# Router output rows kept by partition, loaded with one transfer per group, and added by VectorE alone

## The chip, the cores and the metric

The kernel runs on one core of a Trainium2 chip. The metric is the device time of one execution in microseconds (us); of several runs the median counts. Below, PE is TensorE (matrix products), DVE is VectorE, ACT is ScalarE, POOL is GpSimd and SP is SyncE, which here only issues transfers (DMAs).

## What is computed

The block works on 2048 tokens (8 sequences of 256) of width 128, in float32:

```
x = x + 0.5 * ffn(layernorm(x))        # layer 0: 8 experts, each token goes to 2 of them
x = x + mamba(layernorm(x))            # projections, a short convolution, a scan over time
x = x + 0.5 * ffn(layernorm(x))        # layer 1: the same experts
```

Inside `ffn` a router picks the two best of 8 experts for each token and gives each a weight. With hact = up * gelu(gate), the result of a token is the weighted sum of the two chosen experts' outputs:

```
probs = softmax(x @ gate_w.T); topw, sel = top_k(probs, 2); topw = topw / sum(topw)
out   = sum over the 2 choices of  topw * (hact @ down_w[expert].T)
```

## The kernel before

**Layout.** Token t = 128 c + p lies in partition p and chunk c, so `x` is [128 partitions, 16 chunks, 128]. Four chunks make a group (GROUPS = 4, GC = 4); a group of one tensor is 128 x 512 float32, 256 KB.

**The expert stage.** `route` (DVE, L1033) sorts the 4096 (token, choice) pairs by expert into NT = 39 tiles of 128 places, some of them padding. It builds one-hot matrices; PE (`onehot`, L755) multiplies them with a small constant table (`K_BLOCK`, `K_P`) and gets for each place the block number and the partition of its token. L1093 to L1095 make two row numbers from them: `put_i`, the row of the scratch tensor `expert_rows` in DRAM to which the place's result goes (a number beyond the tensor for padding, which is dropped), and `get_i`, the row of the scratch tensor `xn_rows` in DRAM from which its input comes. SP writes the normalised tokens to `xn_rows` (L327). In `ffn`, POOL issues for each tile one indirect gather (L378, up to six tiles ahead) and one indirect scatter (L386); PE, ACT and DVE do the tile between them. In DRAM, row 128 c + p of `xn_rows` is the token's, and row 2048 k + 128 c + p of `expert_rows` is its choice k: neighbouring rows belong to neighbouring partitions.

**The return.** When all scatters of a layer have landed (L334), SP issues eight loads (L337), for each group g the rows of choice 0 and then those of choice 1, 256 KB each, in runs of 512 bytes. They land in `ybuf[g]`, which shares its space with `ring_space` (groups 0 to 2) and `gate` (group 3); profile rows carry those names. Then ACT scales choice 0 with its weight (L499, four instructions), POOL scales choice 1 (L405, one instruction), and DVE adds both to `x` (L1167, two instructions, the second waits for the first).

**What follows.** After layer 0 DVE's own order is written out by hand: add group 0, statistics of group 0 (L1007 to L1012), add group 1, normalise group 0 (L1023), statistics of group 1, and so on. PE starts matrix products that only keep its clock up (`keep_clock`, L694) when group 0 of `x` is updated, then turns the normalised group 0 (L701), and after ACT's copy (L465) starts the input projection (L865). POOL's queue holds the scalings of layer 0 between its `rsqrt` steps (L363). After layer 1 each group of `x` is stored to the output as soon as it is updated (L340), and the kernel ends.

Of the kernel before, what the change touches and what calls it, by code (L numbers as in the profile page):

```python
# [18 lines left out]
ALU = mybir.AluOpType  # L19
ACT = mybir.ActivationFunctionType  # L20
# [8 lines left out]
P = 128  # L29
B, L, D = 8, 256, 128  # L30
T = B * L
C = T // P
GROUPS, GC = 4, C // 4
GT = GC * P
E, F, TOPK = 8, 512, 2
FC = F // P
J = TOPK * C
NT = (T * TOPK - E) // P + E
# [41 lines left out]
K_BLOCK = K_TILE + NT  # L80
K_P = K_BLOCK + J
# [37 lines left out]
def macaron_block(nc, x_in, experts_in, consts_in, vectors_in, mats_in, out):  # L119
    with ExitStack() as ctx:  # L120
# [3 lines left out]
        def sem(name):  # L124
            return ctx.enter_context(nc.semaphore(name))

        xn_dram = [nc.dram_tensor(f"xn_rows_{l}", (T, D), F32).ap() for l in range(2)]
        y_dram = [nc.dram_tensor(f"expert_rows_{l}", (TOPK * T, D), F32).ap() for l in range(2)]

        ps = ctx.enter_context(nc.psum_tensor("ps", [P, 8, 512], F32))  # L130
# [26 lines left out]
        x = sb("x", [P, C, D])  # L157
# [23 lines left out]
        half_w = sb("half_w", [P, TOPK, C])  # L181
# [18 lines left out]
        put_f = sb("put_f", [P, NT])  # L200
        put_i = sb("put_i", [P, NT], I32)
# [14 lines left out]

        ids = sb("ids", [P, NT])
        gate = sb("gate", [P, T])
        ybuf = [rows.rearrange("p (k c d) -> p k c d", k=TOPK, c=GC) for rows in
                [ring_space[:, i * TOPK * GT:(i + 1) * TOPK * GT] for i in range(3)] + [gate[:, 0:TOPK * GT]]]  # L220

        delta = xn[:].rearrange("p c d -> p (c d)")
# [42 lines left out]
        h_turned, hT_ready = sem("h_turned"), sem("hT_ready")  # L265
        down_done, y_ready = sem("down_done"), sem("y_ready")
        y_loaded = [sem(f"y_loaded_{g}") for g in range(GROUPS)]
        y_scaled = [sem("y_scaled_by_act"), sem("y_scaled_by_pool")]
        x_moved = sem("x_moved")

        xz_done, silu_done, gate_ready = sem("xz_done"), sem("silu_done"), sem("gate_ready")
# [13 lines left out]
        def spread(ap, axis, shape):  # L285
            return ap.unsqueeze(axis).to_broadcast(shape)
# [10 lines left out]
        def grp(g):  # L297
            return slice(g * GC, (g + 1) * GC)
# [12 lines left out]
        @block.sync  # L311
        def _(sp):
            for g in range(GROUPS):
                sp.dma_start(x[:, grp(g), :], x_in[:, grp(g), :]).then_inc(x_loaded[g], 16)
                if g == 1:
                    sp.dma_start(consts[:], consts_in).then_inc(consts_in_s, 16)
            sp.dma_start(mats[:], mats_in).then_inc(mats_in_s, 16)
            for e in range(EARLY_EXPERTS):
                sp.dma_start(w_lo[:, e, :].bitcast(F32), experts_in[:, e, 0:GU]).then_inc(w_loaded[e], 16)

            for l in range(2):
                rows = xn_dram[l].rearrange("(c p) d -> p c d", p=P)
                y_rows = y_dram[l].rearrange("(k c p) d -> p k c d", k=TOPK, p=P)
                for g in range(GROUPS):

                    wait_normalised(sp, 2 * l, g)
                    sp.dma_start(rows[:, grp(g), :], xn[:, grp(g), :]).then_inc(xn_stored[g], 16)  # L327
                if l == 0:
                    for e in range(EARLY_EXPERTS, E):
                        sp.dma_start(w_lo[:, e, :].bitcast(F32), experts_in[:, e, 0:GU]).then_inc(w_loaded[e], 16)  # L330
                    sp.dma_start(w_down[:], experts_in[:, :, GU:WCOLS]).then_inc(down_loaded, 16)
                    sp.dma_start(vectors[:], vectors_in).then_inc(vectors_in_s, 16)
                for r in range(RING):
                    sp.wait_ge(scattered[r], 16 * (l + 1) * PER_SLOT[r])  # L334
                for g in range(GROUPS):
                    for k in range(TOPK):
                        sp.dma_start(ybuf[g][:, k], y_rows[:, k, grp(g), :]).then_inc(y_loaded[g], 16)  # L337
            for g in range(GROUPS):
                sp.wait_ge(x_moved, GROUPS + g + 1)
                sp.dma_start(out[:, grp(g), :], x[:, grp(g), :]).then_inc(stored, 16)  # L340
            sp.wait_ge(stored, 16 * GROUPS)
# [3 lines left out]
        def _(pool):  # L345
# [53 lines left out]
                    if t >= PUT_AFTER:  # L399
                        put(t - PUT_AFTER)  # L400

            def scale_experts(l, g):

                pool.wait_ge(y_loaded[g], 16 * TOPK * (l + 1))
                pool.tensor_tensor(ybuf[g][:, 1], ybuf[g][:, 1],  # L405
                                   spread(half_w[:, 1, grp(g)], 2, [P, GC, D]), ALU.mult).then_inc(y_scaled[1], 1)

            def mamba():
                scale_experts(0, 0)
                scale_experts(0, 1)  # L410
                rsqrt(1, 0)
                scale_experts(0, 2)
                rsqrt(1, 1)
                scale_experts(0, 3)
                rsqrt(1, 2)
                rsqrt(1, 3)

                pool.wait_ge(setup_copied, 3)
                pool.wait_ge(xn_ready, FIRST_ON_ACT + GROUPS)
                pool.tensor_tensor(x[:], x[:], spread(out_c[:], 1, [P, C, D]), ALU.add).then_inc(cb_added, 1)  # L420
                pool.wait_ge(cb_added, 1)
                for q in range(DVE_DELTAS, GROUPS):
                    cols = slice(q * GT, (q + 1) * GT)
                    pool.wait_ge(log_done, q + 1)
                    pool.wait_ge(pos_done, q + 1)
                    pool.tensor_tensor(delta[:, cols], delta[:, cols], soft[:, cols], ALU.add
                                       ).then_inc(pool_delta_ready, 1)
                    pool.wait_ge(pool_delta_ready, q - DVE_DELTAS + 1)
                    pool.tensor_tensor(gate[:, cols], gate[:, cols], delta[:, cols], ALU.mult).then_inc(pool_dg_ready, 1)
                    pool.wait_ge(pool_dg_ready, q - DVE_DELTAS + 1)  # L430

                def step(k, n, ring_new):
                    pool.wait_ge(h_ready, k + 1)
                    pool.wait_ge(c_copied, k + 1)
                    if not ring_new:
                        pool.wait_ge(hc_summed, k - 3)
                    pool.tensor_tensor(hc[:, n % 4, :], hs[:, n % 4, :], c_row[:, n % 4, :],  # L437
                                       ALU.mult).then_inc(hc_ready, 1)

                for n in range(N):  # L440
                    step(n, n, n < 4)
                with pool.Fori(1, GROUPS) as q:
                    for n in range(N):
                        step(q * N + n, n, False)
# [9 lines left out]
            for g in range(GROUPS):  # L454
                rsqrt(2, g)
            ffn(1)
            for g in range(GROUPS):
                scale_experts(1, g)


        @block.scalar
        def _(act):
# [31 lines left out]

            def scale_experts(l, g):

                act.wait_ge(y_loaded[g], 16 * TOPK * (l + 1))
                for c in range(GC):
                    i = nc.scalar.activation(ybuf[g][:, 0, c, :], ybuf[g][:, 0, c, :], ACT.Copy,  # L499
                                             scale=half_w[:, 0, g * GC + c:g * GC + c + 1])  # L500
                i.then_inc(y_scaled[0], 1)

            def load_table(function, i):

# [492 lines left out]
        def _(dve):  # L997
            order = [0]

            def chain(ins):  # L1000
                order[0] += 1
                ins.then_inc(dve_order, 1)
                dve.wait_ge(dve_order, order[0])
# [29 lines left out]
            def route(l):  # L1033
# [56 lines left out]
                dve.tensor_scalar(weights_i[:], exp_f[:], float(E - 1), None, ALU.min)  # L1090

                dve.wait_ge(onehot_used, (l + 1) * GROUPS)
                chain(dve.tensor_scalar(put_f[:], ps[:, 4, 0:NT], float(P), float((J + 1) * P), ALU.mult, ALU.add))  # L1093
                chain(dve.tensor_tensor(put_i[:], put_f[:], ps[:, 4, NT:2 * NT], ALU.add))
                dve.tensor_scalar(get_i[:], put_i[:], T - 1, None, ALU.bitwise_and).then_inc(index_ready, 1)  # L1095

            def second_weights(l):

# [63 lines left out]

            def add_experts(l, g):

                for k in range(TOPK):
                    dve.wait_ge(y_scaled[k], l * GROUPS + g + 1)
                    i = dve.tensor_tensor(x[:, grp(g), :], x[:, grp(g), :], ybuf[g][:, k], ALU.add)  # L1167
                    if k == 0:
                        chain(i)
                i.then_inc(x_moved, 1)  # L1170
                dve.wait_ge(x_moved, l * GROUPS + g + 1)

            def mamba():
# [167 lines left out]
def _constants():  # L1341

    import numpy as np

    k = np.zeros((P, K_COLS), np.float32)
    i = np.arange(P)
    k[:, K_IOTA:K_IOTA + P] = i
    k[:, K_TRI:K_TRI + P] = i[:, None] < i[None, :]
    k[:, K_CENTRE:K_CENTRE + P] = np.eye(P) - 1.0 / P
    k[:, K_IDENT:K_IDENT + P] = np.eye(P)  # L1350
    k[:, K_TILE:K_TILE + NT] = P * np.arange(NT)
    k[:, K_BLOCK:K_BLOCK + J] = np.arange(J) - (J + 1)
    k[:, K_P] = i
    k[:, K_SEL:K_SEL + 2 * N] = (i[:, None] % (2 * N)) == np.arange(2 * N)
    return k

# [28 lines left out]
```

## Time and profile before

| | us |
|---|---|
| median of 3 runs | 534.25 |
| lowest, highest | 532.2, 536.88 |
| the profiled execution | 536.45 |
| its span in the trace | 534.3 |
| PE busy | 445.2 (83%) |
| DVE busy | 309.5 (58%) |
| POOL busy | 276.9 (52%) |
| ACT busy | 253.5 (47%) |

The shares are means over stages with different limits. Layer 0's experts fill about 43 to 172 us, the Mamba block about 172 to 352 us, layer 1's routing and experts about 352 to 517 us, and the last 17 us are the return of layer 1. Only a stretch of the chain that ended last sets the time.

### The profile page before, as it was taken

What the parts mean: (1) busy time and instruction counts of PE and PEld (TensorE: products, weight loads), DVE (VectorE), ACT (ScalarE), POOL (GpSimd) and SP (SyncE); (2) the same over time, 40 slices, a digit from 0 to 9 for tenths busy, and PEclk for the clock granted to TensorE, in tenths of its full rate; (3) what the DMA queues carried; (4) which work ended last, traced back from release to release, by engine and by line L of the source; (5) the groups of instructions that cost most, each with busy time, mean ns of one, the idle gap of its engine ahead of it and who ended that gap; (6) DMA issues with size and microseconds to landing.
All of it is one profiled execution on the core that took longest, in us unless ns stands there. A gap on an engine that the chain in (4) does not pass through costs nothing.

```text
span 534.3 us, 8797 instructions
## 1 busy us (share of the span) xinstructions
PE 445.2 (83%) x2131; PEld 289.2 (54%) x2132; DVE 309.5 (58%) x813; ACT 253.5 (47%) x579; POOL 276.9 (52%) x257
## 2 busy tenths in 40 slices
PE   6977999999997499499898989773989998899940
PEld 3755877787786144032222222422578786777840
DVE  5574433343343654799999999768233443333415
ACT  4474444444354415966666666352134453344413
POOL 3016666666633440377777767630456646665333
PEclk9579999999999589779999999966689999999985
DMA  8901111111200500000000000020011101112026
GB/s 293 373 21 44 40 42 40 42 35 37 41 18 10 157 1 2 0 1 0 2 0 1 0 0 0 2 79 1 25 35 43 45 25 42 36 36 37 23 56 187
DMA packets 21465, 25.01 MB, mean 47 GB/s; under 512 B 3517, under 2 KB 15812, under 8 KB 21440
## 3 DMA queue, kind: packets, MB, share of 16 engines
q1 hardware_dynamic: 16448, 15.39, 8.8%
q0 software_dynamic: 4992, 9.32, 6.6%
q8 instruction: 11, 0.18, 0.1%
q14 instruction: 14, 0.11, 0.1%
HBM read 17.35 MB, written 8.26 MB: 48 GB/s over the span
## 4 chain that ended last, share of the span: by engine, by line
PE 50%; DVE 16%; issue 10%; ACT 10%; another core or an unknown queue 5%; DMA 4%; POOL 2%; SPq 1%; ACTq 0%; DVEq 0%; POOLq 0%
PE ps L817 11%; DVE ring_space L1255 9%; PE ps L788 6%; PE ps L808 6%; PE ps L790 6%; PE ps L789 5%; PE ps L865 3%; DMA ring_space<-expert_rows 2%; ACT shared L615 2%; PE ps L714 2%; PE ps L761 2%; POOL shared L437 2%; PE ps L701 2%; ACT hT L537 1%
## 5 line engine op out<-in xcount | busy, mean ns | idle before, releaser
L378 POOL DMA_INDIRECT xg<-xn_rows,get_i x78 | 80.4, 1031 | 102.8 <-DVE get_i L1095 49.0
L386 POOL DMA_INDIRECT expert_rows<-ysb,put_i x78 | 78.6, 1007 | 57.7 <-DVE ysb L1148 38.1
L1140 DVE TENSOR_TENSOR hidden<-ps,hidden 128x256 f32<-128x256 f32 x156 | 58.8, 418 | 79.2 <-ACT hidden L530 38.9
L437 POOL TENSOR_TENSOR shared<-ring_space,shared 128x512 f32<-128x512 f32 x64 | 82.6, 1292 | 30.9 <-DVE ring_space L1255 30.5
L530 ACT ACTIVATE hidden<-ps 128x256 f32<-128x256 f32 x156 | 52.0, 389 | 80.2 <-PE ps L790 70.1
L817 PE MATMUL ps<-w_down,hT 128*128 x624 | 85.7, 281 | 0.0
L915 PE MATMUL ps<-shared,consts 128*128 128x512 f32 x128 | 73.3, 655 | 9.5 <-POOL shared L437 7.4
L817 PEld LDWEIGHTS ps<-w_down,hT 128*128 128x128 f32 x624 | 76.5, 193 | 3.7 <-issue 0.9
L537 ACT COPY hT<-ps 128x512 f32<-128x512 f32 x78 | 45.7, 586 | 63.5 <-remote 37.6
L788 PE MATMUL ps<-w_hi,xT_hi 128*128 x156 | 68.9, 442 | 4.1 <-issue 3.6
L789 PE MATMUL ps<-w_lo,xT_hi 128*128 x156 | 61.8, 396 | 0.0
L790 PE MATMUL ps<-w_hi,xT_lo 128*128 x156 | 61.8, 396 | 0.0
L808 PE MATMUL ps<-consts,hidden 128*128 128x128 f32 x312 | 48.1, 277 | 10.8 <-ACT hT L537 8.0
L1131 DVE TENSOR_TENSOR xT_lo<-ps,xT_hi 128x128 fp32r<-128x128 f32 x78 | 22.7, 291 | 58.8 <-ACT xT_hi L523 55.5
L615 ACT COPY shared<-ps 128x512 f32<-128x512 f32 x64 | 37.5, 585 | 37.7 <-DVE ring_space L1255 35.4
L808 PEld LDWEIGHTS ps<-consts,hidden 128*128 128x128 f32 x312 | 36.9, 141 | 27.3 <-issue 14.3
L607 ACT ACTIVATE ps<-xn,neg_a 128x510 f32<-128x510 f32 (+1 forms) x64 | 44.5, 696 | 0.0
L915 PEld LDWEIGHTS ps<-shared,consts 128*128 128x128 f32 x128 | 20.3, 194 | 35.5 <-POOL shared L437 32.7
L1255 DVE TENSOR_TENSOR_SCAN ring_space<-ps,ring_space 128x512 f32<-128x512 f32 x32 | 38.9, 1216 | 0.9 <-ACT ps L607 0.9
L1255 DVE TENSOR_TENSOR_SCAN ring_space<-ps,hidden 128x512 f32<-128x512 f32 x32 | 38.8, 1215 | 0.0
L1148 DVE COPY ysb<-ps 128x128 f32<-128x128 f32 x78 | 22.4, 288 | 24.9 <-PE ps L817 19.5
L788 PEld LDWEIGHTS ps<-w_hi,xT_hi 128*128 128x128 f32 x156 | 29.6, 190 | 13.1 <-issue 9.3
(156 smaller groups left out, 609.5 us busy)
## 6 DMA issues: line engine op xcount, KB each, us to landing
w_lo<-in_experts SPq DMA_DIRECT2D x8, 512.0 KB, 7.7
ring_space<-expert_rows SPq DMA_DIRECT2D x12, 256.0 KB, 4.5
xn_rows<-xn SPq DMA_DIRECT2D x8, 256.0 KB, 3.3
w_down<-in_experts SPq DMA_DIRECT2D x1, 2048.0 KB, 11.8
xg<-xn_rows,get_i POOLq DMA_INDIRECT x78
expert_rows<-ysb,put_i POOLq DMA_INDIRECT x78
x<-in_x_rows SPq DMA_DIRECT2D x4, 256.0 KB, 5.1
gate<-expert_rows SPq DMA_DIRECT2D x4, 256.0 KB, 5.4
```

What stands on the lines that cost most here:

```text
L378: pool.indirect_dma_start(out=xg[:, r, :], out_offset=None, in_=xn_dram[l], in_offset=bass.IndirectOffsetOnAxis(ap=get_i[:, t:t + 1].bitca ...
L386: pool.indirect_dma_start(out=y_dram[l], in_=ysb[:, t % RING, :], in_offset=None, out_offset=bass.IndirectOffsetOnAxis(ap=put_i[:, t:t + 1 ...
L437: pool.tensor_tensor(hc[:, n % 4, :], hs[:, n % 4, :], c_row[:, n % 4, :], ALU.mult).then_inc(hc_ready, 1)
L530: nc.scalar.activation(gelu[:, slot % 2, half], ps[:, GATE_BANK[slot % 2], half], ACT.Gelu).then_inc(gelu_done, 1)
L788: pe.matmul(acc, xT_hi[:, slot % 3, :], hi, start=True, stop=False)
L789: pe.matmul(acc, xT_hi[:, slot % 3, :], lo, start=False, stop=False)
L790: return pe.matmul(acc, xT_lo[:, slot % 3, :], hi, start=False, stop=True)
L808: m = pe.transpose(ps[:, HT_BANK, f * P:(f + 1) * P], hact[:, slot % 2, f * P:(f + 1) * P], ident)
L817: m = pe.matmul(ps[:, RESULT_BANK[slot % 2], 0:D], hT[:, slot % 3, f * P:(f + 1) * P], flat_down[:, bass.ds(expert + f * D, D)], start=(f ...
L915: pe.matmul(y_bank(q), ident, hc[:, n % 4, :], start=(n == 0), stop=(n == N - 1)).then_inc(hc_summed, 1)
L1140: dve.tensor_tensor(hact[:, slot % 2, half], ps[:, UP_BANK[slot % 2], half], gelu[:, slot % 2, half], ALU.mult).then_inc(hact_done, 1)
L1255: dve.tensor_tensor_scan(hs[:, n % 4, :], ps[:, DECAY_BANK + n % 2, :], bx[n % 4], 0.0, ALU.mult, ALU.add).then_inc(h_ready, 1)
```

## The change

Both scratch tensors number their rows by partition first: row 16 p + c of `xn_rows`, and row 32 p + 2 c + k of `expert_rows`. A partition's rows of a group are then one run of 2 KB in the first and one of 4 KB, both choices together, in the second. The eight loads of a layer become four of 512 KB. `ybuf[g]` is ordered chunk, choice, column. The constants and L1093 to L1095 are changed so that the row numbers come out in the new order, with as many instructions as before. POOL's scalings are gone. DVE does choice 1 itself: for each chunk one instruction multiplies the row with its weight and adds it to `x` (four of 128 x 128), and then one 128 x 512 addition takes choice 0, scaled by ACT as before. Between these two DVE waits for the first four.

```diff
-        ybuf = [rows.rearrange("p (k c d) -> p k c d", k=TOPK, c=GC) for rows in
+        ybuf = [rows.rearrange("p (c k d) -> p c k d", k=TOPK, c=GC) for rows in
...
-                rows = xn_dram[l].rearrange("(c p) d -> p c d", p=P)
-                y_rows = y_dram[l].rearrange("(k c p) d -> p k c d", k=TOPK, p=P)
+                rows = xn_dram[l].rearrange("(p c) d -> p c d", p=P)
+                y_rows = y_dram[l].rearrange("(p c k) d -> p c k d", k=TOPK, p=P)
...
-                    for k in range(TOPK):
-                        sp.dma_start(ybuf[g][:, k], y_rows[:, k, grp(g), :]).then_inc(y_loaded[g], 16)
+                    sp.dma_start(ybuf[g], y_rows[:, grp(g)]).then_inc(y_loaded[g], 16)
...
-            def scale_experts(l, g):
-
-                pool.wait_ge(y_loaded[g], 16 * TOPK * (l + 1))
-                pool.tensor_tensor(ybuf[g][:, 1], ybuf[g][:, 1],
-                                   spread(half_w[:, 1, grp(g)], 2, [P, GC, D]), ALU.mult).then_inc(y_scaled[1], 1)
-
             def mamba():
-                scale_experts(0, 0)
-                scale_experts(0, 1)
                 rsqrt(1, 0)
-                scale_experts(0, 2)
                 rsqrt(1, 1)
-                scale_experts(0, 3)
...
-                act.wait_ge(y_loaded[g], 16 * TOPK * (l + 1))
+                act.wait_ge(y_loaded[g], 16 * (l + 1))
...
-                chain(dve.tensor_scalar(put_f[:], ps[:, 4, 0:NT], float(P), float((J + 1) * P), ALU.mult, ALU.add))
-                chain(dve.tensor_tensor(put_i[:], put_f[:], ps[:, 4, NT:2 * NT], ALU.add))
-                dve.tensor_scalar(get_i[:], put_i[:], T - 1, None, ALU.bitwise_and).then_inc(index_ready, 1)
+                chain(dve.tensor_scalar(put_f[:], ps[:, 4, NT:2 * NT], float(J), float(J * P), ALU.mult, ALU.add))
+                chain(dve.tensor_tensor(put_i[:], put_f[:], ps[:, 4, 0:NT], ALU.add))
+                dve.tensor_scalar(get_i[:], put_i[:], 1, T - 1, ALU.logical_shift_right, ALU.bitwise_and).then_inc(index_ready, 1)
...
-                for k in range(TOPK):
-                    dve.wait_ge(y_scaled[k], l * GROUPS + g + 1)
-                    i = dve.tensor_tensor(x[:, grp(g), :], x[:, grp(g), :], ybuf[g][:, k], ALU.add)
-                    if k == 0:
-                        chain(i)
-                i.then_inc(x_moved, 1)
+                dve.wait_ge(y_loaded[g], 16 * (l + 1))
+                for c in range(GC):
+                    at = g * GC + c
+                    i = dve.scalar_tensor_tensor(out=x[:, at, :], in0=ybuf[g][:, c, 1, :], scalar=half_w[:, 1, at:at + 1],
+                                                 in1=x[:, at, :], op0=ALU.mult, op1=ALU.add)
+                i.then_inc(second_added, 1)
+                dve.wait_ge(second_added, l * GROUPS + g + 1)
+                dve.wait_ge(y_scaled, l * GROUPS + g + 1)
+                dve.tensor_tensor(x[:, grp(g), :], x[:, grp(g), :], ybuf[g][:, :, 0, :], ALU.add).then_inc(x_moved, 1)
...
-    k[:, K_BLOCK:K_BLOCK + J] = np.arange(J) - (J + 1)
-    k[:, K_P] = i
+    k[:, K_BLOCK:K_BLOCK + J] = np.arange(J).reshape(C, TOPK).T.reshape(J)
+    k[:, K_P] = i - P
```

## Rows read from the trace of the kernel before

**Rows 1.** Chain of waits, 164 to 224 us; columns: start us, us, what.
```profile
170.28 2.13 DMA expert_rows<-ysb,put_i
...
172.53 0.38 SPq L337
...
180.73 0.70 DVE x L1167
...
182.19 1.73 DVE xn L1023 x4
...
185.75 6.74 PE ps L865 x8
```

**Rows 2.** Timeline, 160 to 192 us; start us, us, engine, line, operation, count, idle before.
```profile
176.31 1.28 ACT L499 ACTIVATE ring_space<-ring_space,half_w 128x128 f32<-128x128 f32 x4 [4.38 <-DMA ring_space<-expert_rows]
...
177.62 1.42 DVE L1167 TENSOR_TENSOR x<-x,ring_space 128x512 f32<-128x512 f32 x2 [5.71 <-ACT ring_space L499]
179.07 0.87 DVE L1007 BATCH_NORM_STATS2 stats<-x 128x6 f32<-128x128 f32 x4
...
179.09 4.02 PE L694 MATMUL ps<-ones_b 128*128 128x512 bf16 x9 [7.51 <-DVE x L1167]
...
180.39 0.17 DVE L1012 TENSOR_SCALAR var_e<-mv 128x4 f32<-128x4 f32 x1
180.64 1.04 POOL L363 TENSOR_TENSOR rstd<-var_e,neg_half 128x4 f32<-128x4 f32 x1
...
181.67 1.38 POOL L405 TENSOR_TENSOR ring_space<-ring_space,half_w 128x512 f32<-128x512 f32 x1
...
188.05 1.11 DVE L1023 TENSOR_SCALAR xn<-x,mv,rstd 128x128 f32<-128x128 f32 x4
```

**Rows 3.** Chain of waits, 505 us to the end.
```profile
515.29 2.11 DMA expert_rows<-ysb,put_i
...
525.56 0.70 DVE x L1167
...
526.29 1.42 DVE x L1167
...
527.73 1.48 DVE x L1167
...
530.68 0.69 DVE x L1167
```

**Rows 4.** Timeline, 506 us to the end.
```profile
521.73 1.28 ACT L499 ACTIVATE ring_space<-ring_space,half_w 128x128 f32<-128x128 f32 x4 [9.10 <-DMA ring_space<-expert_rows]
...
526.00 1.15 POOL L405 TENSOR_TENSOR ring_space<-ring_space,half_w 128x512 f32<-128x512 f32 x1 [0.65 <-DMA ring_space<-expert_rows]
...
527.61 1.04 POOL L405 TENSOR_TENSOR gate<-gate,half_w 128x512 f32<-128x512 f32 x1 [0.46 <-DMA gate<-expert_rows]
```

**Rows 5.** Windows: stretch, length, busy of each engine, PEclk, DMA share, GB/s.
```profile
8.00:11.00 3.00, 0.63 (x4) 0.42 (x4) 2.59 (x19) 2.49 (x7) 2.27 (x3) 1.00 1.03 414
...
172.50:174.00 1.50, 0.00 (x0) 0.00 (x0) 0.00 (x0) 0.00 (x0) 0.00 (x0) 1.00 0.05 16
174.00:175.00 1.00, 0.00 (x0) 0.00 (x0) 0.00 (x0) 0.00 (x0) 0.00 (x0) 0.91 1.02 307
175.00:176.00 1.00, 0.00 (x0) 0.00 (x0) 0.00 (x0) 0.00 (x0) 0.00 (x0) 0.50 1.05 276
...
190.00:192.00 2.00, 2.00 (x4) 0.53 0.00 0
...
382.00:384.00 2.00, 2.00 (x9) 0.74 (x6) 0.00 (x0) 0.00 (x0) 1.39 (x3) 0.74 0.11 33
...
100.00:160.00 60.00, 57.69 (x358) 47.77 (x357) 23.95 (x77) 26.25 (x76) 33.68 (x34) 1.00 0.14 34
```

**Rows 6.** One-line views of L1116 and L1255: durations in ns, min/median/max.
```profile
L1116 DVE TENSOR_SCALAR conv_rows<-mats,vectors x4: 277/315/477, 169.2 to 169.7; 128x128 f32<-128x128 f32 x4
...
L1255 DVE TENSOR_TENSOR_SCAN ring_space<-ps,ring_space x32: 1212/1216/1223, 224.2 to 332.9; 128x512 f32<-128x512 f32 x32
```

**Rows 7.** Page, costliest groups: busy us, mean ns, idle before with its releaser.
```profile
L378 POOL DMA_INDIRECT xg<-xn_rows,get_i x78 | 80.4, 1031 | 102.8 <-DVE get_i L1095 49.0
```

More of the change, by code:

```diff
@@ L267, in macaron_block @@
         y_loaded = [sem(f"y_loaded_{g}") for g in range(GROUPS)]
-        y_scaled = [sem("y_scaled_by_act"), sem("y_scaled_by_pool")]
+        y_scaled, second_added = sem("y_scaled"), sem("second_added")
         x_moved = sem("x_moved")
@@ L456, in _ @@
             ffn(1)
-            for g in range(GROUPS):
-                scale_experts(1, g)
         @block.scalar
@@ L495, in scale_experts @@
             def scale_experts(l, g):
-                act.wait_ge(y_loaded[g], 16 * TOPK * (l + 1))
+                act.wait_ge(y_loaded[g], 16 * (l + 1))
                 for c in range(GC):
-                    i = nc.scalar.activation(ybuf[g][:, 0, c, :], ybuf[g][:, 0, c, :], ACT.Copy,
+                    i = nc.scalar.activation(ybuf[g][:, c, 0, :], ybuf[g][:, c, 0, :], ACT.Copy,
                                              scale=half_w[:, 0, g * GC + c:g * GC + c + 1])
-                i.then_inc(y_scaled[0], 1)
+                i.then_inc(y_scaled, 1)
             def load_table(function, i):
```

## Prediction

> **What bounds the kernel now.** I read the page's chain of waits first: half of it is PE, and the scratch loads hold 2%. So the change can act on the path only where the chain passes through them, and I read the chain in detail at those two places, with the timeline beside it for the engines that are not in it.
>
> After layer 0 the chain runs from the last scatter into the loads, then ACT's scaling of group 1, DVE's additions, DVE's normalisation of group 0, and into PE's input projection at 185.75 [rows 1]. From there PE runs through the four groups with only ACT's short copies between, so whatever is won before 185.75 is won for the rest. After layer 1 the chain runs from the last scatter (landed 517.40) into the loads, ACT's scaling of group 1, and then DVE's additions one behind another until 531.37 [rows 3]; the last store and its landing follow.
>
> Two things are to be seen there. First, POOL and DVE slow each other: an addition of 128 x 512 takes 0.70 us, but two single ones that ran beside POOL's scalings took 1.42 and 1.48 [rows 3, 4]. In the same way the normalisation of group 0 took 1.73 beside POOL's scaling (1.38), the next one, mostly alone, 1.11 [rows 1, 2]. Second, the loads in 512-byte runs move 307 and 276 GB/s at their start, while 4 KB runs of the weights moved 414 at the kernel's start [rows 5].
>
> **The change part by part.**
>
> *Loads.* They are issued from 172.53; group 0's first bytes move some 1.35 us later, at about 173.9 (16 GB/s in the mean until 174.00, 307 from there) [rows 1, 5]. Its 0.524 MB take 1.81 us at 290 GB/s and 1.27 at 414, 0.54 less. The bounds are 0 and 0.54; I take 0.45, since the runs are as long as the weights' but strided differently. ACT started at 176.31 and 521.73 [rows 2, 4], so the new starts are 175.86 and 521.28. The later groups (2.10 MB in all) land by about 524.5 after layer 1 (518.85 + 2.10/0.40 + 0.4), or 526.3 at 300 GB/s. Fewer issues on SP cost nothing and free nothing: behind them SP only waits for the output.
>
> *The four new DVE instructions.* The trace has no such instruction on two 128 x 128 tensors. Four 128 x 128 statistics take 0.87 [rows 2]; four scalings with one per-partition factor take 0.93, read from the same timeline (mean start-to-start 0.22, one 0.315) [rows 6]; four with two factors take 1.11 [rows 2]. I take 1.05. Below that the floor is 0.87. The ceiling: the scan of 512 columns takes 1.216 against 0.70 for an addition [rows 1, 6], about 1 ns more per column; with that four would take 0.53 more, 1.58.
>
> The row nearest in kind speaks for one column per cycle (the addition, 0.70 for 512), the scan for two. The Trainium skill has a rule for it: Vector Engine (DVE) Microarchitecture Reference, "Points that are easy to get wrong", says that this instruction form with two SBUF sources that are not bf16 runs at half throughput. By the rule the sum would be the one of the first rival below; no instruction in this trace settles it.
>
> *DVE per group.* Before: 1.42 for two additions. After: 1.05, 0.04 for the wait, one addition 0.70, 0.04: 1.83. DVE has 0.41 more work per group, but no longer starts it after a scaling: the four begin when the load lands, beside ACT's 1.28. In the first group ACT ends last, so x is updated 1.28 + 0.03 + 0.70 = 2.0 after landing.
>
> *After layer 0.* Before: group 0 updated at 179.04 (177.62 + 1.42), statistics to 180.56, wait for ACT's group 1 until 180.73 (its scalings ended at 180.70), additions, normalisation 182.19 to 183.91 [rows 1, 2]. After: 175.86 + 2.0 = 177.87; statistics 1.50 to 179.37 (group 1 has landed by 177.2 even at 300 GB/s plus 0.6); 1.79 to 181.19; POOL's rsqrt, ready 1.1 after the statistics, at 180.5, is in time; normalisation 1.11 without POOL beside it, to 182.34. That is 1.57 earlier: 0.45 load, 0.72 one addition less in group 0, 0.61 the undisturbed normalisation, and -0.21 for group 1. What is next late is nothing on DVE: its later additions have cover, because PE's first projection lasts until 192.5 and needs group 1's normalised rows only then; DVE had them at 189.16 and has them at about 188.4. Were that cover gone, each group would cost 0.41.
>
> *After layer 1.* Start 521.28, first group 2.0 plus 0.03, three more at 1.83: 528.80. DVE sets the end, since all loads have landed before it asks for them. Before 531.37 [rows 3]; gain 2.57. In it are the two slowed additions (0.72 + 0.78 = 1.50).
>
> *Costed at nothing.* The writes of `xn_rows`: the gathers wait for the indices of DVE, not for them [rows 7]. Gathers and scatters in the new row order: POOL issues as many, and PE uses a gather six tiles, some 18 us, after its issue, against some 2.1 us in which a scatter lands [rows 1, 3]; DMA is busy 14% of the expert stage [rows 5]. Only a layer's first gather is nearer its use, where a few tenths could show. The last scatters of a layer (2.13 and 2.11 on the chain [rows 1, 3]) keep their price. Index arithmetic and one-hot products have as many instructions of the same size.
>
> **Sum.** 1.57 + 2.57 = 4.1 us. The profiled span goes from 534.3 to 530.2, its time from 536.45 to about 532.3. That execution lies 2.2 above the median; I subtract from the median: 534.25 - 4.1 = 530.1.
>
> **The rivals.**
>
> *The new instruction at half rate.* Then DVE needs 1.58 instead of 1.05 for the four, and in a first group 0.30 is all that is seen over ACT. Tail: 0.3 + 3 x 0.53 = 1.9 less gain; after layer 0: 0.3 + 0.53 = 0.8 less. Gain 1.4, time 532.9. For it: two operands from SBUF and the scan's row [rows 6]. Against: the addition also has two, at 0.70.
>
> *The clock rises sooner too.* PE starts its projection at half clock (granted 0.50; 0.53 in 190 to 192, so it rose at about 191.9, 6.1 us after 185.75) [rows 1, 5]. Eight instructions took 6.74 there. Before layer 1's experts PE was kept busy from 378.0 and the clock rose at about 383.0 (0.74 in 382 to 384), 5.0 later [rows 5]. With a projection that starts closer behind the `keep_clock` products (4.02 us [rows 2], so from 177.9 to 181.9; the turned group follows at 182.4), the rise may come 3 us sooner relative to the projection, worth half of that, 1.5. Gain 5.6, time 528.6. Against: the gap behind `keep_clock` stays, and where the rise falls may as well be chance.
>
> The Trainium skill (TensorE: Matmul & The Clock Gate, "Part 1") holds that where the rise falls differs from run to run; this trace's two delays, 6.1 and 5.0, agree. By that the forecast keeps its mean and gets wider.
>
> *Slower: the strided long runs load badly.* Every partition's 4 KB run begins 16 KB after its neighbour's. The tail ends at 518.85 + 2.10/rate + 0.4 + 2.0 once loads bind; that is 531.4 at 208 GB/s, where all of the tail's gain is gone. At 150 GB/s the tail loses 3.9 and the stretch after layer 0 0.4: 538.5. It decides from about 200 GB/s. For: nothing loads at this stride now. Against: 512-byte runs of the same tensor reach 276 and 307, long runs 414 [rows 5].
>
> The Trainium skill speaks for it in kind: DMA: Bandwidth & Descriptors, "Latency and other measured facts", gives 207 GB/s for row pitches of 512 KiB, fewer at larger ones, and nothing for 16 KiB. No run here shows it yet.
>
> *It does nothing.* Not possible in full: additions and scalings do leave the chain.
>
> **How the numbers follow.** Forecast 0.55 (its own range, from 0.87 to 1.17 for the four and 0 to 0.54 for the load, gains of 3.1 to 4.8: 529.4 to 531.2). Half rate 0.16. Clock 0.20. Slow loads 0.04. Unforeseen 0.05. The runs before spread over 4.7 us, so a median may be off by 1 to 2 by itself. From the clock case less a little spread to the half rate case: 527.2 to 533.2. About 1%, 5.3 us, is what a measurement of this kernel can tell from no change. Faster by more: the clock case and the upper end of the forecast with favourable spread, 0.28. Slower by more: half of the slow loads and some unforeseen, 0.03. Within 1%: 0.69.
>
> **What would show it.** Right: L1167 once per group at 0.70, never 1.4; the four new instructions at 1.0 to 1.1 per group; the first DVE work of the return 0.4 us sooner after the issue than ACT's was (3.8 and 4.2); last addition at about 11.3 us after the first load's issue instead of 13.8; the chain's tail all DVE. L865 at about 184.2. Half rate: single instructions near 0.42 instead of 0.29. Slow loads: DVE or ACT waiting for a load in group 1 to 3 of the tail, and under 250 GB/s in the windows. Wrong altogether: expert stages longer than before, with PE's L783 waiting for gathers or DVE's L1148 for scatters.

## The result, and the profile after

| | before | changed |
|---|---|---|
| median of 12 runs | 535.45 us | 531.93 us |
| lowest, highest | 532.2, 537.42 | 529.17, 534.5 |
| profiled execution (span) | 536.45 (534.3) | 530.99 (529.1) |

The ratio is 0.9945, with a 95% interval of 0.9923 to 0.9967: 2.9 us faster by it, 3.5 by the medians. That is clear of zero and within 1%. The forecast was 4.1 us and 530.1. It was counted from 534.25, the median of three runs; the twelve runs of the kernel before have 535.45, so 1.2 of the 1.8 us between 530.1 and 531.93 come from the starting point.

The profiled spans differ by 5.2 us. By stage (differences of the times in the traces):

| stretch | before | changed | difference |
|---|---|---|---|
| start to the first load after layer 0 | 172.53 | 174.54 | +2.01 |
| that load's issue to PE's first projection | 13.22 | 12.37 | -0.85 |
| that projection to the first scan | 38.46 | 35.43 | -3.03 |
| first scan to the first load after layer 1 | 293.32 | 291.61 | -1.71 |
| that load's issue to the end of the last addition | 13.85 | 12.29 | -1.56 |
| last addition to the end | 2.92 | 2.86 | -0.06 |

Rows two and five are what the change was costed at. Row three is the clock. Rows one and four are stretches in which the change only reorders scratch rows, and they differ as much between profiles of kernels with the same rows: in nine with the new rows the first load after layer 0 starts between 172.42 and 175.17, in five with the old ones between 172.53 and 173.92; row four is 291.09 to 293.46 long in the four profiles of the kernel before (one of them with 11 clock products), 288.68 to 293.50 in the four of the changed kernel (with 7, 9 and 11).

The changed kernel's return after layer 0, from its chain of waits (start us, us, what); it answers to [rows 1]:

```profile
172.27 2.14 DMA expert_rows<-ysb,put_i
...
174.54 3.99 DMA ring_space<-expert_rows
...
178.55 1.28 ACT ring_space L486 x4
...
179.93 0.70 DVE x L1160
...
182.06 1.14 DVE x L1155 x4
...
183.22 0.70 DVE x L1160
...
183.95 1.12 DVE xn L1010 x4
...
185.12 1.13 PE ps L688 x4
...
186.91 3.70 PE ps L852 x8
```

Read from the top. The normalisation takes 1.12 us, where it took 1.73 beside POOL's scaling. The chain now passes through DVE without a gap from group 0's addition on. And the first eight projection instructions take 3.70 us instead of 6.74.

Its return after layer 1, from the timeline; it answers to [rows 3, 4]:

```profile
513.95 1.27 SPq L336 DMA_DIRECT2D ring_space<-expert_rows  x3
...
518.47 3.83 ACT L486 ACTIVATE ring_space<-ring_space,half_w 128x128 f32<-128x128 f32 x12 [9.43 <-DMA ring_space<-expert_rows]
518.47 1.14 DVE L1155 SCALAR_TENSOR_TENSOR x<-ring_space,half_w,x 128x128 f32<-128x128 f32 x4 [7.81 <-DMA ring_space<-expert_rows]
519.85 0.69 DVE L1160 TENSOR_TENSOR x<-x,ring_space 128x512 f32<-128x512 f32 x1 [0.24 <-ACT ring_space L486]
...
520.58 1.14 DVE L1155 SCALAR_TENSOR_TENSOR x<-ring_space,half_w,x 128x128 f32<-128x128 f32 x4
521.75 0.69 DVE L1160 TENSOR_TENSOR x<-x,ring_space 128x512 f32<-128x512 f32 x1
...
525.55 0.69 DVE L1160 TENSOR_TENSOR x<-x,gate 128x512 f32<-128x512 f32 x1
```

DVE waits for the first load once and never again: four groups of 1.14 + 0.69 and the waits, 7.77 us from its start. ACT's twelve scalings run on without a pause, so groups 1 and 2 had landed before it asked for them. But the start is late, 4.52 us after the issue; before, ACT started 4.20 after it. The windows (stretch, length, busy PE, PEld, DVE, ACT, POOL, PEclk, DMA share, GB/s) show how the loads of the new layout begin after layer 0:

```profile
174.50:176.00 1.50, 0.00 (x0) 0.00 (x0) 0.00 (x0) 0.00 (x0) 0.00 (x0) 1.00 0.26 63
176.00:177.00 1.00, 0.00 (x0) 0.00 (x0) 0.00 (x0) 0.00 (x0) 0.00 (x0) 0.50 0.80 168
177.00:178.00 1.00, 0.00 (x0) 0.00 (x0) 0.00 (x0) 0.00 (x0) 0.00 (x0) 0.50 0.93 344
178.00:179.00 1.00, 0.00 (x0) 0.00 (x0) 0.45 (x2) 0.45 (x2) 0.00 (x0) 0.50 1.03 422
179.00:180.00 1.00, 0.00 (x0) 0.00 (x0) 0.76 (x4) 0.99 (x4) 0.00 (x0) 0.50 1.03 401
```

They do reach 422 GB/s, but only in their fourth microsecond or so; the old runs of 512 bytes were at 307 in their first full one [rows 5]. The long runs win on the sum and lose on the first group. Where they lose it, finer windows show, cut at 1.25, 1.75, 2.5 and 3.0 us after the issue, first the changed kernel, then the one before:

```profile
175.79:176.29 0.50, 0.00 (x0) 0.00 (x0) 0.00 (x0) 0.00 (x0) 0.00 (x0) 0.70 1.04 262
176.29:177.04 0.75, 0.00 (x0) 0.00 (x0) 0.00 (x0) 0.00 (x0) 0.00 (x0) 0.50 0.59 115
177.04:177.54 0.50, 0.00 (x0) 0.00 (x0) 0.00 (x0) 0.00 (x0) 0.00 (x0) 0.50 0.92 328
```

```profile
173.78:174.28 0.50, 0.00 (x0) 0.00 (x0) 0.00 (x0) 0.00 (x0) 0.00 (x0) 1.00 0.47 141
174.28:175.03 0.75, 0.00 (x0) 0.00 (x0) 0.00 (x0) 0.00 (x0) 0.00 (x0) 0.87 1.15 345
175.03:175.53 0.50, 0.00 (x0) 0.00 (x0) 0.00 (x0) 0.00 (x0) 0.00 (x0) 0.50 1.14 342
```

The new loads do not start later; they sag to 115 GB/s for 0.75 us when the old ones run at 345. The sag is there in both returns of all five profiles with runs of 4 KB that were read this way, and in none with runs of 512 bytes; why it comes, no run shows.

### The profile page after: what moved, and what is told of

It is laid out like the page before. It is cut to its first block, busy times and chain, and to the rows that moved or that the text cites. A ratio compares the mean times of both kernels' runs of the same rounds, so it can differ in the third digit from the quotient of the medians.

```text
span 529.1 us, 8805 instructions
## 1 busy us (share of the span) xinstructions
PE 441.9 (84%) x2131; PEld 286.6 (54%) x2132; DVE 310.7 (59%) x837; ACT 253.5 (48%) x579; POOL 267.8 (51%) x249
## 4 chain that ended last, share of the span: by engine, by line
PE 43%; DVE 18%; ACT 12%; issue 11%; another core or an unknown queue 8%; DMA 3%; POOL 2%; ACTq 1%; DVEq 0%; POOLq 0%; SPq 0%
DVE ring_space L1245 10%; PE ps L804 8%; PE ps L777 6%; PE ps L775 5%; PE ps L795 5%; PE ps L776 4%; PE ps L852 3%; PE ps L701 2%; ACT hT L524 2%; ACT shared L602 2%; PE ps L748 2%; ACT hidden L517 2%; POOL shared L426 2%; DMA ring_space<-expert_rows 2%
## 6 DMA issues: line engine op xcount, KB each, us to landing
w_down<-in_experts SPq DMA_DIRECT2D x1, 2048.0 KB, 13.2
```

## The experiments

All medians are beside runs of the kernel before on the same chip. What is compared between kernels is mostly five pieces of the profile, in us: from the first load's issue after layer 0 to the first work on it (start), to PE's turning of the first normalised group (turn), and to PE's first projection; the first eight projection instructions; and from the first load's issue after layer 1 to the end of the last addition (tail). The turning itself took 1.11 where PE was at half clock and 0.66 or less where it was at full clock, so the two columns do not always tell the same. Each row's pieces are those of one execution, its ratio is that of many.

| kernel | ratio (95% interval) | start | turn | to projection | first eight | tail |
|---|---|---|---|---|---|---|
| before | 1 | 3.78 | 11.43 | 13.22 | 6.74 | 13.85 |
| before, second profile | | 3.74 | 11.42 | 12.75 | 5.40 | 13.59 |
| before, third profile | | 3.68 | 11.36 | 13.15 | 6.64 | 13.80 |
| changed | 0.9945 (0.9923 to 0.9967) | 4.01 | 10.58 | 12.37 | 3.70 | 12.29 |
| changed again | 0.9918 (0.9888 to 0.9948) | 4.07 | 10.64 | 12.43 | 3.70 | 11.74 |
| DVE part alone | 0.9931 (0.9901 to 0.9961) | 3.69 | 10.26 | 11.59 | 3.70 | 12.96 |
| layout alone | 0.9988 (0.9962 to 1.0014) | 4.38 | 12.93 | 14.26 | 3.70 | 13.18 |
| two loads per group | 0.9939 (0.9914 to 0.9964) | 3.98 | 10.54 | 11.88 | 3.70 | 11.87 |
| group 0 in halves | 0.9885 (0.9839 to 0.9931) | 3.03 | 10.53 | 11.86 | 5.40 | 11.62 |
| halves, ACT takes the last | 0.9901 (0.9873 to 0.9929) | 3.04 | 10.23 | 11.56 | 3.70 | 12.02 |
| before, 11 products | 0.9970 (0.9947 to 0.9992) | 4.43 | 12.82 | 14.16 | 3.70 | 14.16 |
| changed, 11 products | 0.9924 (0.9903 to 0.9946) | 3.99 | 10.73 | 12.01 | 3.70 | 12.14 |
| changed, 7 products | 0.9951 (0.9928 to 0.9975) | 4.10 | 10.67 | 12.46 | 5.13 | 11.79 |
| halves, 11 products | 0.9905 (0.9870 to 0.9940) | 3.19 | 10.56 | 11.90 | 3.70 | 12.33 |

**The two parts of the change apart.** Theory: the gain comes from taking POOL's scaling away from beside DVE and from starting the return earlier; whether the layout matters on the path was open. The changed kernel was also run again, beside them.

> The changed kernel once more, beside the others on one chip. Theory A (the gain is made of two fixed pieces, and the clock is chance): from the first load's issue to the end of the last addition after layer 1 again about 12.3 us (before: 13.8), from the first load's issue after layer 0 to PE's first projection again about 12.4 (before: 13.2), about 2.4 us faster in the mean; PE's first eight projection instructions anywhere between 3.7 and 6.8 us. Theory B (the change also brings the clock up sooner): these eight at 3.7 to 4.5 us again, and 3.5 us or more faster.

Measured: 528.36 against 532.43. The start (4.07, 3.98 after layer 1) confirms that the first group does not come earlier than with the old layout, and the first eight are at 3.70 again; they and the 4.1 us are what theory B asked for.

The DVE part alone, in the kernel before:

```diff
-                for k in range(TOPK):
-                    dve.wait_ge(y_scaled[k], l * GROUPS + g + 1)
-                    i = dve.tensor_tensor(x[:, grp(g), :], x[:, grp(g), :], ybuf[g][:, k], ALU.add)
+                dve.wait_ge(y_loaded[g], 16 * TOPK * (l + 1))
+                for c in range(GC):
...
+                    i = dve.scalar_tensor_tensor(out=x[:, at, :], in0=ybuf[g][:, 1, c, :], scalar=half_w[:, 1, at:at + 1],
...
+                dve.tensor_tensor(x[:, grp(g), :], x[:, grp(g), :], ybuf[g][:, 0], ALU.add)
...
-                scale_experts(0, 0)
```

> Only the VectorE part: scratch rows and the two loads of 256 KB per group as before, POOL's scalings gone, the four multiply-adds on DVE. Theory A (the gain comes from taking POOL's scaling away beside DVE, the layout brings nothing on the path): tail from issue to last addition 12.4 us, issue to first projection 12.2, so 2.4 us faster than before, as fast as the changed kernel. Theory C (the layout carries a good part, because DVE would otherwise wait for late loads): tail 13.3 or more, 1 us or more slower than the changed kernel.

Measured: 529.07, 3.4 us of the 4.1 that the changed kernel won beside it; the two intervals overlap, so the times do not show that the layout adds anything. But the tail was 12.96, between the two expectations. Its timeline shows why; these are the waits before the second group's work:

```profile
517.46 0.69 DVE L1161 TENSOR_TENSOR x<-x,ring_space 128x512 f32<-128x512 f32 x1 [0.24 <-ACT ring_space L487]
...
519.48 1.14 DVE L1156 SCALAR_TENSOR_TENSOR x<-ring_space,half_w,x 128x128 f32<-128x128 f32 x4 [1.33 <-DMA ring_space<-expert_rows]
```

DVE stands 1.33 us for group 1, which with the old layout lands 7.1 us after the first issue. After that it is never idle for a load. From start to last addition: 9.20 us here, 7.77 with the new layout, so the layout is worth 1.43 in the tail and gives back 0.2 to 0.8 of it by its late start. In the return after layer 0 the statistics lie between group 0 and group 1 and hide that wait; there the layout only costs, 10.26 against 10.58 and 10.64 to the turn, which is the late start of 0.32 to 0.38. To the projection the difference is larger, 11.59 against 12.37 and 12.43, because the turning took 0.66 here and 1.11 in the changed kernel's two profiles: that part is the clock, not the layout.

The layout alone, with POOL's scaling and two additions:

> Only the layout: rows by partition and one load of 512 KB per group, but POOL scales choice 1 and DVE makes two additions as before. Theory A: POOL and DVE still slow each other (single additions of 1.4 us beside POOL's scalings), first DVE work 0.2 to 0.3 us later after the issue than before; tail 13.1, issue to first projection about 13.2: 0.7 us faster than before at most. Theory C: 1.5 us or more faster than before.

Measured: 532.07 against 532.43, no difference clear of noise. The tail is 0.4 to 0.7 shorter than in the three profiles before, 13.18 as expected; the way to the projection is 1.0 to 1.5 longer, which was not expected (13.2). Its timeline after layer 0:

```profile
178.10 1.04 POOL L404 TENSOR_TENSOR ring_space<-ring_space,half_w 128x512 f32<-128x512 f32 x1 [0.19 <-DMA ring_space<-expert_rows]
178.13 2.29 DVE L1166 TENSOR_TENSOR x<-x,ring_space 128x512 f32<-128x512 f32 x2 [6.33 <-ACT ring_space L498]
...
182.02 1.42 POOL L362 TENSOR_TENSOR rstd<-var_e,neg_half 128x4 f32<-128x4 f32 x1 [2.88 <-DVE var_e L1011]
183.43 1.03 POOL L404 TENSOR_TENSOR ring_space<-ring_space,half_w 128x512 f32<-128x512 f32 x1
183.53 1.78 DVE L1022 TENSOR_SCALAR xn<-x,mv,rstd 128x128 f32<-128x128 f32 x4 [0.27 <-POOL rstd L362]
```

Group 1 now lands early, so POOL scales it just while DVE adds group 0: these two additions take 2.29 instead of 1.42 [rows 2]. And POOL's rsqrt, beside DVE's additions, takes 1.42 and is waited for. Neither belongs to the layout alone: the rsqrt took 1.42 in the other two profiles of the kernel before as well, and in its profile with 11 products, whose first work was as late as here (4.43), the two additions took 2.14. So this profile shows how a group that lands soon behind the first brings POOL and DVE together; that the new layout does so more often is argued, not shown. Against the longer way stands an early clock (the first eight at 3.70, about 2.5 us less from projection to first scan than in the mean of the three profiles before). The pieces together would give some 1.9 us, which the interval (up to 2.0) just allows. That the layout pays only without POOL's scaling is not shown by the times either.

**Why the first group lands late.** Each group's load in two transfers of 256 KB with runs of 2 KB:

```diff
-                    sp.dma_start(ybuf[g], y_rows[:, grp(g)]).then_inc(y_loaded[g], 16)
+                    for h in range(2):
+                        sp.dma_start(ybuf[g][:, 2 * h:2 * h + 2],
+                                     y_rows[:, g * GC + 2 * h:g * GC + 2 * h + 2]).then_inc(y_loaded[g], 16)
```

> The changed kernel, but each group's load in two transfers of 256 KB with runs of 2 KB (chunks 0 and 1, then 2 and 3). Theory D (the first group lands late, 4.0 and 4.5 us after its issue, because long runs and transfers of 512 KB let the next groups' data in among the first's): first group 3.4 to 3.8 us after the first issue, and 0.5 us per return won, about 1 us faster than the changed kernel. Theory E (the late first group is the start of the engines on this layout, whatever the size): 4.0 and 4.5 us again, no difference or slightly slower by the longer issue.

Measured: start 3.98 and 3.85, ratio as the changed kernel's. Smaller transfers with shorter runs, changed together, make no difference that these two returns show; what the DMA engines do at the start of the new layout stays open. But the first of the two transfers landed 3.1 and 3.0 us after its issue. So the next kernel waits for it by itself, in group 0 only:

```diff
+                sp.dma_start(ybuf[0][:, 0:2], y_rows[:, 0:2]).then_inc(first_half, 16)
+                sp.dma_start(ybuf[0][:, 2:4], y_rows[:, 2:4]).then_inc(y_loaded[0], 16)
...
+                    if g == 0 and c == 2:
+                        dve.wait_ge(y_loaded[g], 16 * (l + 1))
```

> The changed kernel with group 0's load in two transfers of 256 KB, each with a semaphore of its own, so that ACT and DVE begin on chunks 0 and 1 while 2 and 3 are on their way; groups 1 to 3 as changed. If the returns hang on the first data (DVE busy from it to the end): first work 3.1 us after the issue instead of 4.0, group 0 done 0.6 to 0.7 us sooner, in both returns, 1.3 us faster than the changed kernel. If the second half comes late in turn (behind the start of the engines): 0 to 0.4 us.

Measured: first work at 3.03 and 3.07, as expected; but the second half is waited for (it came 4.5 us after the issue after layer 0), and the turn came only 0.05 to 0.11 sooner than in the changed kernel; that the projection came 0.5 sooner is the turning at full clock. The tail is 0.1 to 0.7 shorter. That fits the second of the two expectations. 4.6 us faster than before by the medians; the intervals of this and the changed kernel overlap, so it is not shown to be better.

> As the one before, and in the last return ACT scales both choices of group 3, so DVE has two additions there (1.42 us) instead of four multiply-adds and an addition (1.87). If DVE alone sets the tail: another 0.45 us, 1.7 us faster than the changed kernel. If ACT's eight scalings end too late (five times 1.28 us from its start, 10.3 us after the issue, beside DVE's 9.2): the second addition waits, and the gain is 0.1 us or none.

Measured: 528.49, and a tail of 12.02, 0.4 longer instead of 0.45 shorter. Two waits eat it, in its timeline:

```profile
515.94 1.14 DVE L1179 SCALAR_TENSOR_TENSOR x<-ring_space,half_w,x 128x128 f32<-128x128 f32 x4 [0.73 <-DMA ring_space<-expert_rows]
...
519.55 1.26 ACT L498 ACTIVATE gate<-gate,half_w 128x128 f32<-128x128 f32 x4
...
520.91 0.69 DVE L1169 TENSOR_TENSOR x<-x,gate 128x512 f32<-128x512 f32 x1 [0.35 <-ACT gate L498]
```

Once group 0 is done sooner, group 1's load is the next thing late (0.73), and ACT's second scaling of the last group ends 0.35 after DVE asks for it.

**The clock.** The profile before had 6.74 us for PE's first eight projection instructions, the next five profiles, of four other kernels, 3.70. Was this chance? Two more profiles of the kernel before:

> The kernel before once more, for its first eight projection instructions. Theory A (where the clock rises is chance): anything between 3.7 and 6.8 us, and the five other profiles so far, all at 3.7, happen to agree. Theory B (the kernel before leaves PE so placed that the clock comes up late): 6 us or more again. Issue to first projection 13.2 and issue to last addition 13.8 by both.

> The same again: theory A 3.7 to 6.8 us for the first eight projection instructions, theory B 6 us or more.

Measured 5.40 and 6.64: above 3.70 in three of three. But 5.40 is less than the 6 that theory B asked for, and all three lie in the range of theory A, so these two alone do not decide. What differs on PE just ahead, from the timelines of PE alone, first the kernel before, then the changed kernel:

```profile
183.96 1.11 PE L701 MATMUL ps<-consts,xn 128*128 128x128 f32 x4 [0.84 <-DVE xn L1023]
185.75 6.74 PE L865 MATMUL ps<-xnT,conv_w 128*128 128x512 f32 x8 [0.68 <-ACT xnT L465]
```

```profile
185.12 1.11 PE L688 MATMUL ps<-consts,xn 128*128 128x128 f32 x4 [0.42 <-DVE xn L1010]
186.91 3.70 PE L852 MATMUL ps<-xnT,conv_w 128*128 128x512 f32 x8 [0.68 <-ACT xnT L452]
```

PE idles 0.84 us behind its clock-keeping products before, 0.42 in the changed kernel. The theory is that this gap decides. The layout alone speaks against its simple form: its gap was 0.93, and its first eight took 3.70. It was tested from both sides, by changing only the number of these products from 9:

```diff
-                keep_clock(9)
+                keep_clock(11)
```

> The kernel before, with 11 instead of 9 products that keep PE's clock up, which fill the gap of 0.84 us before it turns the first normalised group. Theory F (that gap holds the clock down: the three profiles before have 6.74, 5.40 and 6.64 us for the first eight projection instructions): now 3.7 us, and 2 to 3 us faster than before though nothing else is changed. Theory A (chance): 3.7 to 6.8, no faster than before.

> The changed kernel with 11 instead of 9 such products; its gap is 0.42 us. Theory F: the eight at 3.7 us as in two of two profiles with 9; within 0.5 us of the changed kernel, for better (the fewer executions where the clock is late) or worse (at half clock the products end 0.3 us after the normalised group is there). Theory A: the same time.

> The changed kernel with 7 such products, so that its gap is 1.3 us, wider than the one of the kernel before. Theory F: the eight take 5.4 us or more, and the kernel loses 1.5 us or more of its gain (about 1 to 2 us faster than before). Theory A: as fast as the changed kernel.

Measured: the kernel before with 11 has 3.70 and is 1.5 us faster by the medians (ratio 0.9970, interval 0.9947 to 0.9992), less than the 2 to 3 expected. But its gap was not filled:

```profile
181.48 4.02 PE L694 MATMUL ps<-ones_b 128*128 128x512 bf16 x11 [8.89 <-DVE x L1167]
186.37 0.66 PE L701 MATMUL ps<-consts,xn 128*128 128x128 f32 x4 [0.88 <-DVE xn L1023]
187.71 3.70 PE L865 MATMUL ps<-xnT,conv_w 128*128 128x512 f32 x8 [0.68 <-ACT xnT L465]
```

The clock rose 3.0 us after the first product, so the 11 took no longer than the 9 at half clock, and the gap is 0.88. The changed kernel with 7 has a gap of 1.27 us and 5.13:

```profile
185.84 1.11 PE L688 MATMUL ps<-consts,xn 128*128 128x128 f32 x4 [1.27 <-DVE xn L1010]
187.63 5.13 PE L852 MATMUL ps<-xnT,conv_w 128*128 128x512 f32 x8 [0.67 <-ACT xnT L452]
```

and it is only 1.8 us faster than before, where with 11 it is 3.7 us faster beside it and with 9 it was 4.1 and 3.5: more products than 9 win nothing there. All fourteen profiles by their gap, the last kernel below included:

| gap, us | profiles | first eight |
|---|---|---|
| none to 0.42 | changed, changed again, DVE part alone, two loads per group, changed with 11, halves with 11 | 3.70 in all six |
| 0.84 and 0.87 | before, before (third) | 6.74, 6.64 |
| 0.88 to 0.93 | before with 11, halves with ACT taking the last, layout alone | 3.70 in all three |
| 1.00 to 1.34 | halves, changed with 7, before (second) | 5.40, 5.13, 5.40 |

So a short gap always went with the early clock and a gap of 1.0 and more never did; at 0.9 it went both ways. What differs there is when the clock rose: in the three with 3.70 it rose 2.9 to 3.8 us after the first product, while PE was still at the products; in the other two it had not risen when they ended, and came 12.8 and 12.6 after the first. In the halves kernel and the second profile before it also rose early, after 2.7 and 2.9, and fell again after 6.1 and 6.4, behind gaps of 1.00 and 1.34. Why it rises at one time or another in the same kernel these runs do not show. The theory is left in a weaker form: by these fourteen a short gap makes the early clock likelier. That two more products gain time is shown by the medians; by which way, in the kernel before, is not. The last kernel puts the halves and the 11 together:

> The changed kernel with group 0's load in two halves (as before in this study) and 11 instead of 9 products that keep the clock up. With 9 its profile had a gap of 1.0 us, because PE ran them at full clock, and 5.40 us for the first eight projection instructions. Theory F: 3.7 us, issue to first projection 11.6 to 12.0, issue to last addition 11.6; 5 to 6 us faster than before. Theory A: no better than with 9, 4.5 us faster at most.

Measured: 3.70 instead of 5.40 as expected, but 529.13 against 533.52, 4.4 us, less than the 5 to 6 expected and no more than theory A allowed. Its tail was 12.33 in the profile, not 11.6: DVE waited 0.93 us for group 1 there, after 0.31 with 9 products. It is as fast as the changed kernel and the other versions; which of them is fastest these runs do not tell.

## Why the prediction was right, and where it was off

**The places and the direction were right.** Both returns became shorter and DVE sets the tail's end: the additions are single ones of 0.69 to 0.70, the slowed ones of 1.42 and 1.48 are gone.

**The load term had the wrong sign.** The prediction took 0.45 us off each start, by weighing the rate of long runs (414) against short ones (290). The rate came (422), but not at the start. First work came 3.98 to 4.52 us after the issue in the changed kernel's two profiles, 3.67 to 4.20 in three profiles before. In place of -0.45 stands about +0.3 per return. The step that failed is the use of a rate read in mid-stream for the first half megabyte after a pause: the rows of before had no long runs starting from rest. What came instead is the sag to 115 GB/s, 1.75 to 2.5 us after the issue.

**The four new instructions** took 1.14 us, against 1.05 taken and 0.87 to 1.17 as the near range. One takes 0.345 to 0.352 us alone, and their starts lie 0.27 apart. The half rate rival had 1.58, and near 0.42 for a single one. The Trainium skill's rule of half throughput for this form with two float32 SBUF sources (Vector Engine (DVE) Microarchitecture Reference, "Points that are easy to get wrong") isn't borne out here; the measurement decides. No run has this form wider than 128 columns, so how its time splits into a fixed part and a rate is not shown.

**The sums.** Tail: 2.57 forecast, 1.56 and about 2.1 measured in the two profiles of the changed kernel. To PE's first projection: 1.57 forecast, 0.85 and 0.79. Together 2.4 to 2.9 instead of 4.1; the missing part is the load term, 0.7 to 0.8 in three of the four returns and 0.2 in the fourth, and 0.09 per group for the new instructions. The forecast's own range, gains of 3.1 to 4.8, was also narrower than its bounds: all low ends together give about 2.8, all high ones about 5.0.

**The clock rival held in part.** The prediction gave it 0.20 as chance on top of the forecast, and 1.5 us, and named against it that the gap behind the clock-keeping products stays. The gap did not stay, it halved, and the first eight took 3.70 in both profiles of the changed kernel. How much of the gain this is stays open. In the profiles the stretch from the first projection to the first scan is 38.46, 37.12 and 38.36 before and 35.43 twice after, 2.5 us in the mean; but with the 2.4 to 2.9 from the returns that is 4.9 to 5.4, more than the 2.9 to 4.1 of the many runs. What these leave beside the returns is 0 to 1.7. The runs with another count put it at 1.5 in the kernel before (0.4 to 2.8 by the interval) and at 1.7 to 2.3 in the changed one. About 1 us is an estimate from these. It came near to the forecast because an overrated term and an underrated one offset each other, and that was luck.

**The slow-load rival** did not come in the sum: 400 GB/s at this stride. The Trainium skill's warning on row pitches (DMA: Bandwidth & Descriptors, "Latency and other measured facts") begins at 512 KiB, and at 16 KB nothing of the kind is seen.

**Costed at nothing, rightly as far as seen:** the last scatter still lands 2.14 and 2.12 us after its issue, and DMA is busy 14% of the expert stage in both.

## What to carry to other kernels

Ask of a layout change what it does to the first bytes after a pause, not only to the rate: the consumer starts on the first group. Where two engines slow each other, making their input arrive sooner need not help: the layout alone won nothing that could be measured. Take the conflict away first. And look at PE's small gaps just ahead of a long stretch of PE work: with gaps up to 0.42 us the clock was up for it in six profiles of six, with longer ones in three of eight.

## What was not expected of the hardware

- A gap of 0.84 and 0.87 us between two bursts of PE work, after 4.0 us of products, went with a late clock in two profiles of the kernel before; in the third, PE had its clock early (2.9 us after the first product), ran the products in 3.55 us, idled 1.34 and fell back to half clock for part of the projection (5.40). With 0.42 the clock rose 5.6 and 5.5 us after the first product in the two profiles of the changed kernel, before the projection began. Gaps of 0.88 to 0.93 behind an early rise did it no harm in three profiles.
- Loads with 4 KB runs of the layout tried moved 63, 168, 344 and 422 GB/s in successive windows after the issue; those with 512-byte runs 16 and then 307 [rows 5]. Between 1.75 and 2.5 us after the issue the long runs sag to 115. Halving the transfers did not change when a whole group had landed (3.98 against 4.07 us).
- POOL's tiny rsqrt (128 x 4) takes 1.04 us alone, and 1.38 to 1.42 where it starts during DVE's additions of two SBUF tensors.
